# Attention softmax denominators: how the probability blocks are summed before TensorE counts them

## The chip, the cores and the metric

One core of a Trainium2 chip runs one program: a whole decoder layer. The metric is the time of the device in microseconds (us). The kernel before takes 5530.57 us, the median of three runs (5529.32 to 5534.97).

## What is computed

The reference is a decoder layer on x of 2 x 2048 x 512 in float32: self-attention after a layer norm, cross-attention to 77 context rows, and a feed-forward part whose operands are quantised in blocks. The change touches the self-attention alone. It has 16 heads of width 32 and, for every head, two softmaxes with the same queries: a short one with a decay bias and a long one without.

```python
def _attention(q, k, v, bias):
    hd = q.shape[-1]
    scores = jnp.einsum('bhqd,bhkd->bhqk', q, k) / jnp.sqrt(jnp.float32(hd))
    if bias is not None:
        scores = scores + bias[None, None]
    attn = jax.nn.softmax(scores, axis=-1)
    return jnp.einsum('bhqk,bhkd->bhqd', attn, v)
...
decay_bias = -jnp.abs(pos[None, :] - pos[:, None]) * (1.0 - decay_factor)
out_short = _attention(q, k_s, v_s, decay_bias)
out_long = _attention(q, k_l, v_l, None)
out = alpha * out_short + (1.0 - alpha) * out_long
```

With 2 batches, 16 heads and 2 softmaxes there are 64 attention units of 2048 x 2048 scores.

## The kernel before

The program has three stages: the projections (to about 630 us of the span), the attention, which is the function `attend` (about 630 to 4190 us), and the finish (the rest). Only `attend` is changed.

**Units, passes, steps.** A pass has `UNITS` = 4 units (two heads, each with its short and its long softmax), and there are `PASSES` = 16: the first and the last are written out, the others are a hardware loop. A unit has `KB` = 16 blocks of 128 keys, and for each block all 2048 queries stand in `NQ` = 4 chunks of 512. TensorE takes a unit in 16 steps, i = 0 to 15. Each engine has its own instruction stream and runs it in order; they meet at semaphores. A `Rises` object holds a semaphore and how often it rises in a pass.

**One step of TensorE** (the loop over i at the end of the function):
- `times_v(w, n, i)`, L907: the values of block i times its probabilities, into `outputs_T`; first it waits for the exponentials of the block (`expd`).
- `count`, L917, in 6 of the 16 steps: a 128 x 32 tile of ones times a 128 x 2048 tile of summed probabilities, accumulated in `sums`; this is the softmax denominator.
- four `scores_for_exp` (keys by queries, tile `scores_kq`, two banks), for the second half of the next block and the first half of the one after it, and four `scores_for_max` (queries by keys, tile `scores_qk`, three banks) of a later unit, interleaved. The matrix products are at L836.

**The other engines.** ScalarE takes the exponential of each chunk of `scores_kq` into `probs_T` (L745), a ring of `PBUF` = 8 blocks of 128 x 2048 float32. Before it fills a block's buffer again it waits until that block has been used by `times_v` (`summed`) and by the summing (`added`). VectorE reduces each chunk of `scores_qk` to a row maximum (L764), 64 chunks a unit. At the unit's end it negates the maxima (L769), TensorE turns them (`turn_max`, L878), ScalarE rounds them (`round_max`, L719), and SyncE copies them by DMA as one more row of the query operand (`place_max`, L632), where the first `scores_for_exp` of the next unit needs them.

**The summing.** GpSimd adds probability blocks in groups, so that `count` has one tile to multiply in place of two or three:

```python
GROUPS = ((0, 1, 2), (3, 4, 5), (6, 7, 8), (9, 10, 11), (12, 13), (14, 15))
COUNT_LAG = 3
```

A group of three is two adds of 128 x 2048 (L704), a group of two is one: 10 adds and 6 counts a unit. The sum of a group goes to one of two buffers (`probs_group_sum`), and it is counted `COUNT_LAG` = 3 steps after its last block: in steps 5, 8, 11, 14 and, for the last two groups, in steps 0 and 2 of the next unit.

**The end of a unit.** ScalarE copies `sums` out (`take_sums`, L724) when it comes to block 4 of the next unit. VectorE inverts it in four pieces of 128 x 128 (`invert`, L786) in steps 3 to 6 (`INVERT` = 3), multiplies in step 8 (`weigh`, L792) and adds the two softmaxes of a head in step 10 (`mix`, L799). It copies the unit's output out in step 15 (`take`, L781). SyncE stores the mix and, when a unit's last scores are done, loads the operands of the same slot for the next pass (`load`, L619 to L625).

**The maxima's lead.** `ASTEPS` = 12: in steps 0 to 11 the `scores_for_max` and their reductions belong to the last 12 blocks of the next unit, in steps 12 to 15 to the first 4 blocks of the unit after that. The maxima of a unit are thus complete after step 11, and `turn_max` stands in step 12 (`TURN_MAX`). Ahead of the first unit the prologue does all 64 chunks of unit 0 and `EARLY` = 16 chunks of unit 1.

Of the kernel before, what the change touches and what calls it, by code (L numbers as in the profile page):

```python
# [16 lines left out]
F32 = mybir.dt.float32  # L17
# [7 lines left out]
P = 128  # L25
# [487 lines left out]
ASTEPS = 12  # L513

TURN_MAX = 12
INVERT = 3
WEIGH = 8
MIX = 10


GROUPS = ((0, 1, 2), (3, 4, 5), (6, 7, 8), (9, 10, 11), (12, 13), (14, 15))
COUNT_LAG = 3
GROUPS_N = len(GROUPS)
ADDS = KB - GROUPS_N


def adds_until(kb):

    return sum(max(0, sum(b <= max(kb, g[1]) for b in g) - 1) for g in GROUPS if g[0] <= kb)

# [11 lines left out]
def attend(nc, qk_scr, v_scr, gates, kinkA, kinkB, pos_scr, attn_scr):  # L542
# [4 lines left out]
    with ExitStack() as ctx:  # L547
# [10 lines left out]
        group_sum = sb("probs_group_sum", [P, 2, L], F32)  # L558
# [32 lines left out]
        counted = Rises(sem("a_counted"), UNITS * GROUPS_N, credit=1)  # L591
# [89 lines left out]
        def _(pool):  # L681
            give_credit(pool, [maxed, expd, summed, added, counted, taken, sums_out, weighed] + stored)
# [7 lines left out]

            def one_pass(n):
                for w in range(UNITS):
                    for g, blocks in enumerate(GROUPS):

                        wait_apart(pool, counted, counted.at(n, w * GROUPS_N + g - 1), passed)
                        total = group_sum[:, g % 2, :]
                        for b in blocks[1:]:

                            wait_apart(pool, expd, expd.at(n, (w * KB + b + 1) * NQ), passed)
                            first = probs[:, blocks[0] % PBUF, :]  # L700
                            if b > blocks[1]:
                                first = total
                                wait_apart(pool, added, added.at(n, w * ADDS + adds_until(b) - 1), passed)
                            nc.gpsimd.tensor_tensor(total, first, probs[:, b % PBUF, :], ALU.add).then_inc(added.sem, 1)  # L704
# [5 lines left out]
        def _(act):  # L710
# [17 lines left out]
            def one_pass(n, first, last):  # L728
                for w in range(UNITS):
                    back = unit_before(w, n, first)  # L730
                    for kb in range(KB):

                        if back and kb == COUNT_LAG + 1:
# [5 lines left out]
                        old = w * KB + kb - PBUF  # L739
                        act.wait_ge(summed.sem, summed.at(n, old + 1))  # L740
# [649 lines left out]
```

## Time and profile before

The profiled execution took 5527.18 us, of which the span of the profile is 5525.4 us. That is 3.39 us below the median of the three runs.

| | share of the span busy | in the attention |
|---|---|---|
| TensorE | 96% | bound of nearly every step |
| VectorE | 75% | about four fifths |
| ScalarE | 52% | about two thirds |
| GpSimd | 53% | 640 adds of about 4.5 us, otherwise nearly nothing |
| the 16 DMA engines | 11% (by their data queue) | a burst at each unit's end |

How to read the rows: engines are PE (TensorE matrix products), PEld (its weight loads), DVE (VectorE), ACT (ScalarE), POOL (GpSimd) and SP (SyncE, SPq its DMA queue). A name such as L907 is a line of the kernel. In a row of a timeline the first two numbers are start and duration in us, "x8" says how many instructions are merged in it, and the bracket tells how long the engine sat idle before it and what released it. Busy time of PE is not PE at its peak, since matrix products are pipelined.

### The profile page before, as it was taken

What the parts mean: (1) busy time and instruction counts of PE and PEld (TensorE: products, weight loads), DVE (VectorE), ACT (ScalarE), POOL (GpSimd) and SP (SyncE); (2) the same over time, 40 slices, a digit from 0 to 9 for tenths busy, and PEclk for the clock granted to TensorE, in tenths of its full rate; (3) what the DMA queues carried; (4) which work ended last, traced back from release to release, by engine and by line L of the source; (5) the groups of instructions that cost most, each with busy time, mean ns of one, the idle gap of its engine ahead of it and who ended that gap; (6) DMA issues with size and microseconds to landing.
All of it is one profiled execution on the core that took longest, in us unless ns stands there. A gap on an engine that the chain in (4) does not pass through costs nothing. (4 is left out here: it accounts for less than half of the span.)

```text
span 5525.4 us, 97876 instructions
## 1 busy us (share of the span) xinstructions
PE 5303.8 (96%) x28780; PEld 2173.6 (39%) x28780; DVE 4137.8 (75%) x7218; ACT 2882.7 (52%) x5201; POOL 2944.0 (53%) x658
## 2 busy tenths in 40 slices
PE   7999899999999999999999999999996999999999
PEld 3444333333333333333333333333333555555555
DVE  5334688878887888878788878787873777777777
ACT  1111166666666666666666666666663333333332
POOL 0000088888888888888888888888882000000000
PEclk9999799999999999999999999999998999999999
DMA  4332301010101010101001010101001000000000
GB/s 136 107 102 88 92 19 34 21 29 22 34 22 29 22 33 22 29 24 32 25 26 32 24 29 21 34 21 29 21 5 47 23 17 23 17 22 18 17 23 12
DMA packets 145582, 191.11 MB, mean 35 GB/s; under 512 B 18500, under 2 KB 97988, under 8 KB 145030
## 3 DMA queue, kind: packets, MB, share of 16 engines
q1 hardware_dynamic: 145159, 185.65, 11.3%
q8 instruction: 243, 3.98, 0.3%
q14 instruction: 180, 1.47, 0.1%
HBM read 123.56 MB, written 61.64 MB: 34 GB/s over the span
## 5 line engine op out<-in xcount | busy, mean ns | idle before, releaser
L764 DVE TENSOR_REDUCE rowmax_parts<-scores_qk 128x1 f32<-128x512 f32 x4096 | 2529.9, 681 | 642.2 <-PE scores_qk L836 642.2
L745 ACT ACTIVATE probs_T<-scores_kq 128x512 f32<-128x512 f32 x4096 | 2279.8, 597 | 1178.1 <-PE scores_kq L836 1115.7
L704 POOL TENSOR_TENSOR probs_group_sum<-probs_T 128x2048 f32<-128x2048 f32 x384 | 1744.3, 4542 | 563.3 <-ACT probs_T L745 563.3
L836 PE MATMUL scores_kq<-q_operand,k_operand 103*128 103x512 f16 (+3 forms) x3712 | 1274.2, 349 | 10.2 <-ACT probs_T L745 8.3
L704 POOL TENSOR_TENSOR probs_group_sum<-probs_group_sum,probs_T 128x2048 f32<-128x2048 f32 x256 | 1194.4, 4666 | 45.7 <-POOL probs_group_sum L704 45.7
L836 PE MATMUL scores_qk<-k_operand,q_operand 96*128 96x512 f16 (+4 forms) x3712 | 1120.0, 351 | 25.0 <-DMA k_operand<-positions_dram 18.9
L907 PE MATMUL outputs_T<-probs_T,v_operand 128*32 128x512 f32 x8192 | 1093.5, 606 | 28.1 <-issue 24.1
L836 PEld LDWEIGHTS scores_kq<-q_operand,k_operand 103*128 103x128 f16 x3712 | 358.4, 97 | 916.1 <-ACT probs_T L745 522.6
L1339 PE MATMUL f_gate_up<-w_gate_up,xq_T 128*128 128x352 f32 x2048 | 627.3, 462 | 0.8 <-issue 0.8
L836 PEld LDWEIGHTS scores_qk<-k_operand,q_operand 96*128 96x128 f16 (+1 forms) x3712 | 354.5, 98 | 401.2 <-DVE rowmax_parts L764 147.1
L1339 PEld LDWEIGHTS f_gate_up<-w_gate_up,xq_T 128*128 128x128 f32 x2048 | 382.6, 190 | 202.3 <-issue 2.8
L917 PE MATMUL sums<-probs_group_sum,ones 128*32 128x512 f32 x3072 | 415.6, 594 | 13.3 <-issue 10.5
L836 PE MATMUL scores_kq<-q_operand_above,k_operand 103*128 103x512 f16 (+3 forms) x1152 | 398.4, 346 | 0.8 <-ACT probs_T L745 0.6
L836 PE MATMUL scores_qk<-k_operand,q_operand_above 102*128 102x512 f16 (+3 forms) x1152 | 372.8, 352 | 11.1
L473 PE MATMUL products_p<-xn_T,w_qkv 128*128 128x512 f32 x768 | 335.6, 592 | 0.8 <-ACT xn_T L418 0.8
L1328 PE MATMUL f_gate_up<-w_down,hidden_T 128*128 128x512 f32 x704 | 332.5, 599 | 3.4 <-DVE hidden L1247 2.7
L683 POOL MEMSET ones<- 128x32 f32 x1 | 0.1, 125 | 602.4 <-POOLq L213 602.4
L907 PEld LDWEIGHTS outputs_T<-probs_T,v_operand 128*32 128x32 f32 x8192 | 161.3, 108 | 314.1 <-issue 266.6
L786 DVE RECIPROCAL sums_inverse<-sums_T 128x128 f32<-128x128 f32 x256 | 241.0, 943 | 16.2 <-ACT sums_T L724 16.2
L836 PEld LDWEIGHTS scores_kq<-q_operand_above,k_operand 103*128 103x128 f16 x1152 | 110.1, 96 | 345.4 <-ACT probs_T L745 234.1
L494 PE MATMUL products_p<-w_qkv,xn_T 128*128 128x512 f32 x512 | 221.1, 592 | 0.0
L473 PEld LDWEIGHTS products_p<-xn_T,w_qkv 128*128 128x128 f32 x768 | 143.7, 190 | 171.0 <-issue 171.0
(144 smaller groups left out, 3608.2 us busy)
## 6 DMA issues: line engine op xcount, KB each, us to landing
qk_parts_dram<-qk_parts SPq DMA_DIRECT2D x96, 256.0 KB, 2.5
q_operand<-qk_parts_dram SPq DMA_DIRECT2D x192, 128.0 KB, 2.5
k_operand<-qk_parts_dram SPq DMA_DIRECT2D x192, 128.0 KB, 3.0
v_dram<-v_heads SPq DMA_DIRECT2D x16, 1024.0 KB, 5.5
v_operand<-v_dram SPq DMA_DIRECT2D x64, 256.0 KB, 3.3
q_operand_above<-qk_parts_dram SPq DMA_DIRECT2D x96, 128.0 KB, 2.8
x_groups<-x SPq DMA_DIRECT2D x8, 1024.0 KB, 8.8
attention_dram<-o_mixed SPq DMA_DIRECT2D x128, 64.0 KB, 1.6
```

The source lines that it names most:

```text
L473: last = nc.tensor.matmul(mm[:, m % 4, :], w[:, c, m * P:(m + 1) * P], xT[:, u, c, :], start=c == 0, stop=c == KT - 1)
L494: last = nc.tensor.matmul(mm[:, j % 4, :], xT[:, u, c, t * P:(t + 1) * P], w[:, c, (3 + a) * H:(4 + a) * H], start=c == 0, stop=c == KT - 1)
L683: nc.gpsimd.memset(ones[:, :], 1.0).then_inc(consts, 1)
L704: nc.gpsimd.tensor_tensor(total, first, probs[:, b % PBUF, :], ALU.add).then_inc(added.sem, 1)
L745: nc.scalar.activation(probs[:, kb % PBUF, qt * BANK:(qt + 1) * BANK], pb[:, k % 2, :], ACT.Exp)\
L764: nc.vector.reduce_max(rowmax[:, w % 2, c // NQ, c % NQ:c % NQ + 1], pa[:, k % 3, :], AX.X)\
L786: nc.vector.reciprocal(inv[:, r * P:(r + 1) * P], sums[:, r * P:(r + 1) * P]).then_inc(inverted.sem, 1)
L836: return nc.tensor.matmul(out, lhsT, rhs, start=start, stop=stop, skip_group_check=True)
L907: last = nc.tensor.matmul(po[qt * HD:(qt + 1) * HD, :], v_op[:, w, kb, :], probs[:, kb % PBUF, qt * BANK:(qt + 1) * BANK], start=kb == 0, ...
L917: last = nc.tensor.matmul(pc[qt * HD:(qt + 1) * HD, :], ones[:, :], group_sum[:, g % 2, qt * BANK:(qt + 1) * BANK], start=g == 0, stop=g = ...
L1328: last = nc.tensor.matmul(pg[:, 0, 0, :], hT[:, c, :], wd[:, c, :], start=c == 0, stop=c == FT - 1)
L1339: last = nc.tensor.matmul(pg[:, k % 2, g, 0:FW], xqT[:, t, c, :], wgu[:, c, g, k * FW:(k + 1) * FW], start=c == 0, stop=c == KT - 1)
```

## The change

Blocks 0, 1, 3, 5, 7, 9, 11, 13 and 14 of a unit are summed by GpSimd in 8 adds into one tile (two buffers, taken in turn by the units). The other seven are summed by DMAs which GpSimd issues and which add into their destination: chain 0 takes blocks 2, 6 and 10, chain 1 takes blocks 4, 8, 12 and 15. The first DMA of a chain is a plain copy of its block, each later one waits for the one before it and then adds its block. Each moves 128 x 2048 float32, 1 MiB, from one on-chip buffer to another. The three tiles are counted in step 14 (chain 0), step 17, that is step 1 of the next unit (GpSimd's tile), and step 19, that is step 3 of the next unit (chain 1): 3 counts in place of 6.

ScalarE, before it fills a buffer again, waits for the add or for the landing of the DMA that used the block. `take_sums` moves from block 4 to block 5, the inversions from steps 3 to 6 to steps 5 to 8, `weigh` from 8 to 10, `mix` from 10 to 11. `ASTEPS` and `TURN_MAX` go from 12 to 10, which puts `round_max` from block 14 to block 12 and makes `EARLY` 24 chunks in place of 16.

```diff
-ASTEPS = 12
-TURN_MAX = 12
-INVERT = 3
-WEIGH = 8
-MIX = 10
-GROUPS = ((0, 1, 2), (3, 4, 5), (6, 7, 8), (9, 10, 11), (12, 13), (14, 15))
-COUNT_LAG = 3
+ASTEPS = 10
+TURN_MAX = 10
+INVERT = 5
+WEIGH = 10
+MIX = 11
+BY_POOL = (0, 1, 3, 5, 7, 9, 11, 13, 14)
+BY_DMA = ((2, 6, 10), (4, 8, 12, 15))
+ADDS = len(BY_POOL) - 1
+POURS = [len(blocks) for blocks in BY_DMA]
+COUNT_POURED = (14, KB + 3)
+COUNT_ADDED = KB + 1
+TAKE_SUMS = 5
...
+            def add(w, n, b):
+                total = added_sum[:, w % 2, :]
+                wait_apart(pool, expd, expd.at(n, (w * KB + b + 1) * NQ), passed)
+                if b == 1:
+                    first = probs[:, 0, :]
+                    wait_apart(pool, counted, counted.at(n, w - 1), passed)
+                else:
+                    first = total
+                    wait_apart(pool, added, added.at(n, w * ADDS + adds_until(b) - 1), passed)
+                nc.gpsimd.tensor_tensor(total, first, probs[:, b % PBUF, :], ALU.add).then_inc(added.sem, 1)
+            def pour(w, n, b, c):
+                i = BY_DMA[c].index(b)
+                wait_apart(pool, expd, expd.at(n, (w * KB + b + 1) * NQ), passed)
+                if i == 0:
+                    wait_apart(pool, counted_poured[c], counted_poured[c].at(n, w), passed)
+                    nc.gpsimd.dma_start(poured_sum[c][:, :], probs[:, b % PBUF, :]).then_inc(poured[c].sem, 16)
+                else:
+                    wait_apart(pool, poured[c], poured[c].at(n, w * POURS[c] + i), passed)
+                    nc.gpsimd.dma_start(poured_sum[c][:, :], probs[:, b % PBUF, :], accum_op=ALU.add)\
+                        .then_inc(poured[c].sem, 16)
...
+                    for b in range(1, KB):
+                        if b in BY_POOL:
+                            add(w, n, b)
+                        else:
+                            pour(w, n, b, int(b in BY_DMA[1]))
...
-                act.wait_ge(counted.sem, counted.at(n, (w + 1) * GROUPS_N))
+                act.wait_ge(counted_poured[1].sem, counted_poured[1].at(n, w + 1))
...
+                        if b in BY_POOL:
+                            act.wait_ge(added.sem, added.at(n, u * ADDS + adds_until(b)))
+                        elif u >= 0 or not first:
+                            c = int(b in BY_DMA[1])
+                            act.wait_ge(poured[c].sem, poured[c].at(n, u * POURS[c] + BY_DMA[c].index(b) + 1))
...
+            def count_poured(w, n, c):
+                if c == 0:
+                    pe.wait_ge(sums_out.sem, sums_out.at(n, w))
+                pe.wait_ge(poured[c].sem, poured[c].at(n, (w + 1) * POURS[c]))
+                count(poured_sum[c], counted_poured[c], c == 0, c == 1)
+            def count_added(w, n):
+                pe.wait_ge(added.sem, added.at(n, (w + 1) * ADDS))
+                count(added_sum[:, w % 2, :], counted, False, False)
```

## Rows read from the trace of the kernel before

**Rows 1.** The page: busy time, share of span and instructions; then busy tenths.

```profile
PE 5303.8 (96%) x28780; PEld 2173.6 (39%) x28780; DVE 4137.8 (75%) x7218; ACT 2882.7 (52%) x5201; POOL 2944.0 (53%) x658
...
PE   7999899999999999999999999999996999999999
```

**Rows 2.** Windows of 500 us: length, each engine's busy us (instructions), TensorE clock, DMA.

```profile
2000.00:2500.00 500.00, 490.63 (x3242) 165.72 (x3237) 405.62 (x652) 330.00 (x603) 419.00 (x92) 1.00 0.10 27
3500.00:4000.00 500.00, 490.90 (x3233) 164.64 (x3230) 407.34 (x656) 331.17 (x606) 421.22 (x93) 1.00 0.09 26
```

**Rows 3.** Timeline of PE, lines 907 and 917: steps 1 to 6 of a unit.

```profile
2002.50 1.07 PE L907 MATMUL outputs_T<-probs_T,v_operand 128*32 128x512 f32 x8
...
2005.45 1.07 PE L907 MATMUL outputs_T<-probs_T,v_operand 128*32 128x512 f32 x8
2006.34 1.04 PE L917 MATMUL sums<-probs_group_sum,ones 128*32 128x512 f32 x8
...
2009.36 1.06 PE L907 MATMUL outputs_T<-probs_T,v_operand 128*32 128x512 f32 x8
...
2012.56 1.06 PE L907 MATMUL outputs_T<-probs_T,v_operand 128*32 128x512 f32 x8
...
2015.75 1.06 PE L907 MATMUL outputs_T<-probs_T,v_operand 128*32 128x512 f32 x8
...
2019.65 1.06 PE L907 MATMUL outputs_T<-probs_T,v_operand 128*32 128x512 f32 x8
```

**Rows 4.** The page's costliest groups: the counts.

```profile
L917 PE MATMUL sums<-probs_group_sum,ones 128*32 128x512 f32 x3072 | 415.6, 594 | 13.3 <-issue 10.5
```

**Rows 5.** One line, L781, once a unit: duration min/median/max, first and last start.

```profile
L781 DVE COPY o_T<-outputs_T x64: 691/692/693, 744.2 to 4175.1; 128x512 f32<-128x512 f32 x64
```

**Rows 6.** Timeline of DVE in the same steps as Rows 3.

```profile
2007.96 2.48 DVE L764 TENSOR_REDUCE rowmax_parts<-scores_qk 128x1 f32<-128x512 f32 x4 [1.33 <-PE scores_qk L836]
2010.36 0.94 DVE L786 RECIPROCAL sums_inverse<-sums_T 128x128 f32<-128x128 f32 x1
2011.22 2.42 DVE L764 TENSOR_REDUCE rowmax_parts<-scores_qk 128x1 f32<-128x512 f32 x4
2013.55 0.94 DVE L786 RECIPROCAL sums_inverse<-sums_T 128x128 f32<-128x128 f32 x1
```

**Rows 7.** One line, L704, over the attention: duration in ns, first and last start.

```profile
L704 POOL TENSOR_TENSOR probs_group_sum<-probs_T x384: 4517/4543/4557, 696.9 to 4174.0; 128x2048 f32<-128x2048 f32 x192
L704 POOL TENSOR_TENSOR probs_group_sum<-probs_group_sum,probs_T x256: 4515/4538/4978, 701.6 to 4162.6; 128x2048 f32<-128x2048 f32 x128
```

**Rows 8.** Timeline around a unit's end: the maxima's row, and step 15 at 2210.14.

```profile
2202.82 0.24 ACT L719 CAST negmax_T<-turned 16x128 f16<-16x128 f32 x1
...
2203.09 0.53 SPq L632 DMA_DIRECT2D q_operand<-negmax_T  x1
...
2209.86 4.52 POOL L704 TENSOR_TENSOR probs_group_sum<-probs_T 128x2048 f32<-128x2048 f32 x1 [2.21 <-ACT probs_T L745]
...
2210.14 1.06 PE L907 MATMUL outputs_T<-probs_T,v_operand 128*32 128x512 f32 x8
```

**Rows 9.** DMA issues by line: count, KB each, median us from issue to landing.

```profile
v_dram<-v_heads SPq DMA_DIRECT2D x16, 1024.0 KB, 5.5
...
x_groups<-x SPq DMA_DIRECT2D x8, 1024.0 KB, 8.8
...
w_qkv<-L_attn_Wkv_long SPq DMA_DIRECT2D x2, 1024.0 KB, 13.4
...
q_operand<-negmax_T SPq DMA_DIRECT2D x64, 4.0 KB, 1.7
```

**Rows 10.** Window of the loads at the start, and timeline of two DMA issues.

```profile
5.00:20.00 15.00, 0.00 (x0) 0.00 (x0) 14.03 (x16) 0.00 (x0) 0.00 (x0) 1.00 1.04 385
...
619.57 3.92 SPq L340 DMA_DIRECT2D v_dram<-v_heads  x2
629.13 1.28 SPq L619 DMA_DIRECT2D q_operand<-qk_parts_dram  x3
```

**Rows 11.** Timeline: the prologue's 64 reductions, and the attention's last add and count.

```profile
642.01 38.36 DVE L764 TENSOR_REDUCE rowmax_parts<-scores_qk 128x1 f32<-128x512 f32 x64 [8.46 <-PE scores_qk L836]
...
4173.92 1.07 PE L907 MATMUL outputs_T<-probs_T,v_operand 128*32 128x512 f32 x8 [0.96 <-ACT probs_T L745]
4174.05 4.52 POOL L704 TENSOR_TENSOR probs_group_sum<-probs_T 128x2048 f32<-128x2048 f32 x1 [2.08 <-ACT probs_T L745]
...
4178.62 1.07 PE L917 MATMUL sums<-probs_group_sum,ones 128*32 128x512 f32 x8 [2.77 <-POOL probs_group_sum L704]
```

More of the change, by code:

```diff
@@ L511 @@
 MROW = PARTS3 + NPOS
[L513 to L524 removed]
+ASTEPS = 10
[10 more added lines that the diff above has]
+TAKE_SUMS = 5
 def adds_until(kb):
[L529 removed]
+    return max(1, BY_POOL.index(kb))
 def chunks_of(i):
@@ L557, in attend @@
         probs = sb("probs_T", [P, PBUF, L], F32)
-        group_sum = sb("probs_group_sum", [P, 2, L], F32)
+        added_sum = sb("probs_added", [P, 2, L], F32)
+        poured_sum = [sb(f"probs_poured{i}", [P, L], F32) for i in range(2)]
         rowmax = sb("rowmax_parts", [P, 2, KB, NQ], F32)
@@ L590, in attend @@
         added = Rises(sem("a_added"), UNITS * ADDS, credit=1)
-        counted = Rises(sem("a_counted"), UNITS * GROUPS_N, credit=1)
+        poured = [Rises(sem(f"a_poured{i}"), UNITS * POURS[i], 16) for i in range(2)]
+        counted = Rises(sem("a_counted"), UNITS, credit=1)
+        counted_poured = [Rises(sem(f"a_counted_poured{i}"), UNITS, credit=1) for i in range(2)]
         taken = Rises(sem("a_o_taken"), UNITS, credit=1)
@@ L731, in one_pass @@
                     for kb in range(KB):
-                        if back and kb == COUNT_LAG + 1:
+                        if back and kb == TAKE_SUMS:
                             take_sums(*back)
@@ L909, in times_v, with count, counts @@
                 last.then_inc(summed.sem, 1)
-            def count(w, n, g):
-                if g == 0:
-                    pe.wait_ge(sums_out.sem, sums_out.at(n, w))
-                pe.wait_ge(added.sem, added.at(n, w * ADDS + adds_until(GROUPS[g][-1])))
-                for qt in range(NQ):
-                    last = nc.tensor.matmul(pc[qt * HD:(qt + 1) * HD, :], ones[:, :], group_sum[:, g % 2, qt * BANK:(qt + 1) * BANK],
-                                            start=g == 0, stop=g == GROUPS_N - 1)
-                last.then_inc(counted.sem, 1)
+            def count(src, done, first, last):
+                for qt in range(NQ):
+                    mm = nc.tensor.matmul(pc[qt * HD:(qt + 1) * HD, :], ones[:, :], src[:, qt * BANK:(qt + 1) * BANK],
+                                          start=first, stop=last)
+                mm.then_inc(done.sem, 1)
+            def count_poured(w, n, c):
+                if c == 0:
+                    pe.wait_ge(sums_out.sem, sums_out.at(n, w))
+                pe.wait_ge(poured[c].sem, poured[c].at(n, (w + 1) * POURS[c]))
[3 more added lines that the diff above has]
+                count(added_sum[:, w % 2, :], counted, False, False)
+            def counts(w, n, i):
+                for c in range(2):
+                    if i == COUNT_POURED[c]:
+                        count_poured(w, n, c)
+                if i == COUNT_ADDED:
+                    count_added(w, n)
             for c in range(CHUNKS):
@@ L947, in maxima @@
                                 scores_for_max(*unit, chunks[c])
-                        due = [(u, g) for g in range(len(GROUPS)) for u, d in (((w, n), 0), (back, KB))
-                               if u and GROUPS[g][-1] + COUNT_LAG == i + d]
                         times_v(w, n, i)
-                        for u, g in due:
-                            count(*u, g)
+                        counts(w, n, i)
+                        if back:
+                            counts(*back, KB + i)
                         scores(i + 1, 2)
@@ L969, in _ @@
             end = (UNITS - 1, PASSES - 1)
-            for g in range(GROUPS_N):
-                if GROUPS[g][-1] + COUNT_LAG >= KB:
-                    count(*end, g)
+            for i in range(KB):
+                counts(*end, KB + i)
 CTX, CD = 77, 1024
```

17 lines of the change are left out of this document (3 added, 14 removed).

## The prediction

> **What bounds the kernel now.** I read the page first. TensorE is busy for 96% of the span and its row of tenths stays at 9 through the attention [rows 1], so the question is whether a TensorE instruction taken out there is time taken out. The windows of the steady stretch say nearly the same: in 500 us PE is busy 491, DVE 406 to 407, ACT 330 and POOL 419 to 421, at the full granted clock, and the DMA engines are a tenth busy [rows 2]. No engine but PE is close to the bound on average, and the DMA engines are nearly free.
>
> Then the timeline of PE, which is a ruler: each step begins with the eight products of L907. From 2002.50 to 2005.45 is a step without a count, 2.95 us; from 2005.45 to 2009.36 is one with a count, 3.91 us [rows 3]. The count starts 0.89 us after the step and the products after it are moved by its own length. Compared with the usual steps without a count, 2.95 to 3.05, I take 0.87 us for what a count adds. The page's group of the counts gives the same scale: 415.6 us for 3072 products, 8 to a count, so 384 counts of 1.08 us busy each, of which the pipelining hides a part [rows 4]. The first and last of the 64 copies of L781 are 3430.9 us apart [rows 5]; over 63 units that is 54.5 us a unit. Some of it is lost at the loop's back edge; a common unit has 10 steps without and 6 with a count, 10 x 3.05 + 6 x 3.87 = 53.7 us.
>
> Next DVE in the same steps. In the steps that begin at 2009.36 and 2012.56, which last 3.20 and 3.19 us without a count, DVE runs without a gap: an inversion starts at 2010.36, four reductions at 2011.22, the next inversion at 2013.55 [rows 3, 6]. The pitch is 3.19 us: 0.86 for the inversion and 2.33 for four reductions. So these steps, and only these, are set by DVE; PE is late there by 0.15 to 0.25 us.
>
> **The change, part by part.** *Counts taken out.* Three a unit, 192 in all, by 0.87 us: -167 us. All of it lies on the path, since PE sets the steps in which they stand, except what the next paragraph gives back.
>
> *Inversions moved to steps 5 to 8, no count among them.* Before, steps 3, 4 and 6 had no count but step 5 had, and a count step of 3.9 us covers the 3.19 of DVE. Now all four steps last at least 3.19. Four times 0.2 above a step of 2.99, less the 0.45 or so that the old kernel paid in steps 3, 4 and 6, is +0.4 us a unit, +26 us. `weigh` and `mix` (a little under 0.7 us each by the copy of the same shape [rows 5]) make a DVE step of 2.33 + 0.69 = 3.0, about PE's own, so I cost their move at nothing; the cover is thin. The ends are 0 and 1.0 us a unit, the latter if the banks of `scores_qk` never recover between steps 5 and 11. DVE's total is no bound: 406/500 of 54.5 is 44 us of work for a unit.
>
> *GpSimd's adds.* 8 by 4.54 us is 36.3 us a unit where it was 10 [rows 7]. What a DMA issued from GpSimd costs that engine, the trace does not show. The nearest rows are issues from SyncE: 0.43 us each for small ones, 1.96 us each for 1 MiB stores [rows 10]. Nothing makes it less than zero, since the instruction is new. I take 1.2, between them, so 36.3 + 7 x 1.2 = 44.7 of a unit of 51.4 us (53.7 - 2.6 + 0.4 = 51.5; I carry 51.4). GpSimd stays under the bound up to (51.4 - 36.3)/7 = 2.16 us an issue.
>
> *The chains.* This is the part on which the forecast hangs. A block's exponentials are complete about 0.3 us before its step starts: GpSimd was released for block 15 at 2209.86, and step 15 starts at 2210.14 [rows 8]. In the new order GpSimd adds block 11 from 0.3 us before step 11 for 4.54 us, and comes to the DMA of block 12 at 1.2 us after the start of step 12. Steps 12 to 14 (the last with a count) last 10.0 us. Blocks 13 and 14 are two adds in a row, from 0.3 us before step 13, which end 1.9 us after the start of step 15; there GpSimd comes to the DMA of block 15. The count of chain 1 follows `times_v` of step 19, which is 12.9 + 0.9 = 13.8 us after the start of step 15. Let D be the time from when GpSimd begins a DMA to its landing. If D is up to 10.7 the DMA of block 15 is not held by that of block 12, and it lands by 12.6, before 13.8. If D is longer it waits for block 12's, both run in series, and it lands at 2D - 8.8 on that scale, so PE waits 2D - 22.6 us a unit once D is over 11.3. Chain 0 and the other links have four steps, over 12 us, and its count in step 14 comes four steps after block 10, so they bind later.
>
> D has no row of its own. 1 MiB lands in 5.5 us (16 stores), 8.8 us (8 loads of x) and 13.4 us (two weight loads with six others in flight) [rows 9]. An accumulating DMA reads its destination as well. With all engines busy the loads at the start moved 385 GB/s [rows 10], so one more MiB read is 2.7 us. I take 5.5 + 2.7 + 1.2 for the issue, 9.4 us: it fits, with 1.3 us to spare at the link from 12 to 15. I lean to the 5.5 because the stores were packets of a source that stands in the core's memory, as here, and because few other transfers are in flight. The ends are 5.5 and 14.6 (13.4 + 1.2). By the same rate five accumulates (5.4 us) and two copies (2.7 us) keep the DMA engines busy 32.4 us of 51.4, beside the tenth that they were.
>
> The Trainium skill speaks against this part, in "Collectives: The Full Stack", section "The bandwidth ceiling: the fold count and why AG ≠ RS ≠ AR": a reducing DMA has two reads for one write on the same read ring, and so moves data at half the rate of a copy. Applied to the mere extra MiB that is what I have done; applied to the whole of the 8.8 us row it would be 17.6 us, well past 11.3. No row here shows a reducing DMA.
>
> *Buffers and maxima.* ScalarE now waits for a DMA's landing before it fills a buffer, eight blocks later, over 24 us after the block's exponentials: hidden by the ring, unless D passes 20 us. `round_max` ran at 2202.82 and its DMA was issued at 2203.09, to land 1.7 us later, for scores at about 2209.5 in step 14 [rows 8, 9]: some 4.5 us to spare. Two steps earlier makes it over 10; this covers the case that the 4 KB row queues behind a 1 MiB DMA. SyncE's queue has this DMA first, then `store`, then `load`, and none comes later than before, since `mix` moves one step within a unit. `take_sums` comes one block later and its count one step later, so no inversion waits that did not.
>
> *Once per kernel.* The prologue has 8 more reductions at 38.36/64 = 0.6 us: +5 us [rows 11]; what the end of the last pass but one gives back is under 1 us. At the very end the last add was done 4.7 us after the start of step 15, and then came the count [rows 11]. Now block 15's DMA begins at about 2.8 on that scale and lands 9.4 later, 12.2: +8, minus the count of the add that is over by then, so +7 to +9; I take 9.
>
> The sum: -167 + 26 + 5 + 9 = -127 us. The profiled execution took 5527.2 us, so 5400.2; the median stands 3.4 us above it, so **5404 us**. Its own range is 5369 (no loss at DVE, no tail) to 5450 (a loss of 1.0 us a unit there, +38, and a few us for the first and last units).
>
> **The rivals.**
> *The chain lands late (0.22).* This ends slower. The place is the count of chain 1 in step 3 of the next unit. The units give back 2.2 us each and PE waits 2D - 22.6, so it decides at D = 12.4; at the 14.6 of the longest row the wait is 6.6 us a unit, 422 us, and the time 5404 + 422 = 5826. For it: a second read, two chains in flight at once, the 8.8 and 13.4 us rows. Against it: the DMA engines are idle for nine tenths, and the longer rows are loads in a crowd. The skill's rule above, taken in full, is this rival's case.
> *GpSimd becomes the bound (0.09).* An issue over 2.16 us fills it, over (53.7 - 36.3)/7 = 2.49 us it is slower than before. At 3.0 the unit is 57.3 us, 5.9 above 51.4, so 5404 + 378 = 5782. For it: descriptors for 128 rows have to be made by an engine which never made any here. Against it: both issue rows are under 2.
> *Little is gained (0.09).* DVE and a chain that is late by a microsecond eat most of the 2.2 us a unit: 5450 to 5540, about 5490 in the middle. For it: DVE alone sets the inversion steps. Of this, 0.05 is faster and 0.04 within 0.2%.
> That the change does not do what it says would mean that PE does not win the count's time; the two kinds of step, 2.95 and 3.91 us, leave no room for it.
>
> **How the numbers follow.** Forecast 0.60, late chain 0.22, GpSimd 0.09, little gained 0.09. Faster by over 0.2%: 0.60 + 0.05 = 0.65; within 0.2%, about what a measurement of this kernel can tell from no change: 0.04; slower: 0.31. The range: below 5372 I leave 0.03. Above, the late chain reaches 5700 at D = 13.6 and GpSimd at 2.8 us; I put 0.12 of the one and 0.05 of the other beyond. So 5372 to 5700, with 0.20 outside. As both signs have weight: the likeliest case alone has 5369 to 5450.
>
> **What would show it.** Right: copies of L781 about 51.4 us apart, steps of 3.2 us at 5 to 8, the count in step 19 with no wait on a DMA, GpSimd with gaps before most adds, D under 11. Late chain: PE idle before the second poured count, released by a DMA, and GpSimd waiting on a landing before block 15's. GpSimd bound: its adds back to back with the issues, PE waiting on adds or ScalarE on buffers, steps long everywhere. Wrong would be the forecast if D or the issue is out of its bounds, or if GpSimd's adds, 4.54 us with no such DMA beside them, get longer.

## The result and the profile after

The changed kernel takes 5347.05 us (median of four, 5345.61 to 5348.42) against 5530.59: a ratio of 0.9666, 95% interval 0.9652 to 0.9681, or 183.5 us less. The forecast was 5404 us, which is 127 us less, with a range down to 5372. The sign was right, the gain was 57 us larger than forecast, and the measured time lies 25 us below the range. The kernel before took 5528.0 to 5530.6 us (medians) in each of the five sets of runs, so times of different sets are put beside each other as they are.

The page after, busy time and share of span; then the queues (packets, MB, share of 16 engines), and the groups of the DMA issues and their landing (KB each, median us). They answer to [rows 1] and [rows 9]:

```profile
PE 5140.3 (96%) x27244; PEld 2119.3 (40%) x27244; DVE 4123.0 (77%) x7218; ACT 2889.4 (54%) x5201; POOL 2657.0 (50%) x978
...
q0 software_dynamic: 64512, 469.79, 37.8%
q1 hardware_dynamic: 145159, 185.65, 11.5%
...
L718 POOL DMA_DIRECT2D probs_poured<-probs_T x320 | 276.8, 865 | 0.0
...
probs_poured<-probs_T POOLq DMA_DIRECT2D x448, 1024.0 KB, 7.3
```

PE is the bound as before. The DMA engines are busy for 38% of the span more, and issuing an accumulating DMA keeps GpSimd 0.865 us. The line of the page on L718 holds the 320 accumulates; the 128 copies stand at L715. The two lines by themselves, with the time from issue to landing (min/median/max):

```profile
L718 POOL DMA_DIRECT2D probs_poured<-probs_T x320: 826/864/906, 719.1 to 3989.6; - x160
DMA to landing us min/median/max: 6.9/7.6/10.6
```
```profile
L715 POOL DMA_DIRECT2D probs_poured<-probs_T x128: 583/593/738, 706.6 to 3955.2; - x128
DMA to landing us min/median/max: 4.4/4.6/6.0
```

So D, the quantity on which the forecast hung, is 7.6 us (median) for an accumulate and 4.6 for a copy: the accumulate takes 3.0 us more.

The steady window, which answers to [rows 2] (length, PE, PEld, DVE, ACT, POOL busy with instructions, clock, DMA share, GB/s), and one line, the copy that is made once a unit, which answers to [rows 5]:

```profile
2000.00:2500.00 500.00, 494.90 (x3194) 167.02 (x3196) 431.38 (x698) 352.66 (x643) 404.20 (x146) 1.00 0.71 170
```
```profile
L808 DVE COPY o_T<-outputs_T x64: 691/692/694, 747.1 to 3987.9; 128x512 f32<-128x512 f32 x64
```

PE is busy 495 of 500 us, DVE 431, and the DMA share is 0.71 where it was 0.10. From the first to the last of these copies it is 3240.8 us, and was 3430.9.

**Where the 180.8 us of the two spans went.** I took the distance of each of those 64 copies from the next. Common units lasted 53.2 and 54.0 us in turn and now last 51.1 and 51.8. Besides, every fourth unit, the one that holds the back edge of the loop over the passes, lasted 57.4 to 59.5 us and now lasts 52.1 or 52.2. There are 13 such edges. The time in them above a unit of 54.01 or 51.77 us was 55.7 us in all and is 4.8. So:

| part of the span | before | after | difference |
|---|---|---|---|
| to the first copy | 744.2 | 747.1 | +2.9 |
| 13 back edges, above a common unit | 55.7 | 4.8 | -50.9 |
| the 63 units without that | 3375.2 | 3236.0 | -139.2 |
| from the last copy on | 1350.3 | 1356.7 | +6.4 |

The third row is 2.2 us a unit, as forecast. The second row is the part that the forecast did not have. What follows is mostly about it.

### The profile page after: what moved, and what is told of

It reads as the page before. It is cut to its first block and busy times, and to the rows that moved or that the text cites. A ratio compares the mean times of both kernels' runs of the same rounds, so it can differ in the third digit from the quotient of the medians.

```text
span 5344.6 us, 96126 instructions
## 1 busy us (share of the span) xinstructions
PE 5140.3 (96%) x27244; PEld 2119.3 (40%) x27244; DVE 4123.0 (77%) x7218; ACT 2889.4 (54%) x5201; POOL 2657.0 (50%) x978
## 5 line engine op out<-in xcount | busy, mean ns | idle before, releaser
L707 POOL TENSOR_TENSOR probs_added<-probs_added,probs_T 128x2048 f32<-128x2048 f32 x448 | 2030.1, 4532 | 461.0 <-ACT probs_T L772 449.6
L863 PE MATMUL scores_kq<-q_operand,k_operand 103*128 103x512 f16 (+3 forms) x3712 | 1274.6, 349 | 10.6 <-ACT probs_T L772 8.7
L934 PE MATMUL outputs_T<-probs_T,v_operand 128*32 128x512 f32 x8192 | 1091.9, 605 | 4.9 <-ACT probs_T L772 4.9
L707 POOL TENSOR_TENSOR probs_added<-probs_T 128x2048 f32<-128x2048 f32 x64 | 290.3, 4536 | 242.4 <-ACT probs_T L772 242.4
L934 PEld LDWEIGHTS outputs_T<-probs_T,v_operand 128*32 128x32 f32 x8192 | 161.2, 108 | 295.8 <-issue 228.1
L718 POOL DMA_DIRECT2D probs_poured<-probs_T x320 | 276.8, 865 | 0.0
```

The lines of the kernel that those rows point to most:

```text
L718: nc.gpsimd.dma_start(poured_sum[c][:, :], probs[:, b % PBUF, :], accum_op=ALU.add)\
L863: return nc.tensor.matmul(out, lhsT, rhs, start=start, stop=stop, skip_group_check=True)
L934: last = nc.tensor.matmul(po[qt * HD:(qt + 1) * HD, :], v_op[:, w, kb, :], probs[:, kb % PBUF, qt * BANK:(qt + 1) * BANK], start=kb == 0, ...
```

## The experiments

### The back edge: code or work?

Timeline of PE at a back edge of the kernel before, from step 15 (2210.14) to step 1 of the next pass:

```profile
2210.14 1.06 PE L907 MATMUL outputs_T<-probs_T,v_operand 128*32 128x512 f32 x8
2215.48 1.06 PE L907 MATMUL outputs_T<-probs_T,v_operand 128*32 128x512 f32 x8 [2.25 <-issue]
2216.36 1.02 PE L917 MATMUL sums<-probs_group_sum,ones 128*32 128x512 f32 x2
2218.51 1.06 PE L917 MATMUL sums<-probs_group_sum,ones 128*32 128x512 f32 x6 [1.13 <-issue]
2221.47 1.06 PE L907 MATMUL outputs_T<-probs_T,v_operand 128*32 128x512 f32 x8
```

PE waits twice, and for nothing that the profile shows ("issue"): 2.25 us at the edge, and 1.13 us in the middle of a count. The same place in the kernel after:

```profile
2135.80 1.06 PE L934 MATMUL outputs_T<-probs_T,v_operand 128*32 128x512 f32 x8
2139.21 1.07 PE L934 MATMUL outputs_T<-probs_T,v_operand 128*32 128x512 f32 x8 [0.32 <-ACT probs_T L772]
2142.17 1.06 PE L934 MATMUL outputs_T<-probs_T,v_operand 128*32 128x512 f32 x8
```

Both waits on issue are gone. Theory 1: they come from where the loop's instructions lie in TensorE's stream. Theory 2: they come from the work around the edge, which the change also moved (a count in step 0, the maxima, the DMAs).

To place the code I counted TensorE's instructions in the built program, two to a float16 product and four to a float32 one, and took the remainder by 256. The body of the loop begins at 0.82 of such a stretch in the kernel before and its branch stands at 0.09; in the kernel after it is 0.14 and 0.60.

**Padding the kernel before.** The edit is the same in all paddings, with other numbers and, where "hidden", ahead of the prologue, where PE idles while operands load. Two waits are one instruction:

```diff
+            for _ in range(128):
+                pe.wait_ge(consts, 4)
             with nc.Fori(1, PASSES - 1, engines=[pe.engine], hint_back_edge=True) as n:
```

> The kernel before with 64 instructions put into TensorE's stream just ahead of its loop over the passes, each a wait that is already fulfilled; nothing else is changed. Theory 1 (code fetch): in the kernel before, PE stands idle for some 4.4 us at each of the 14 back edges because of where the loop's code lies; by the program the loop body of before begins 0.82 of the way through a stretch of 256 instructions and its branch stands 0.09 into one, in the kernel after it is 0.14 and 0.60. The padding makes it 0.07 and 0.34. Expected: the unit that spans the edge falls from about 58 to 54 us and the time by about 58 us, to 5473 us (the padding itself costs under 10 us). Theory 2 (order of work at the edge: a count in step 0, loads of operands): the padding changes nothing, 5531 to 5540 us.

Measured: 5487.1 us, ratio 0.9923 (0.9906 to 0.9939). The units at the edge last 54.4 or 54.5 us. The unit in which the padding runs lasts 8.8 us longer, 0.14 us an instruction; without it the gain would be 51 us. (The expectations speak of 14 edges; the loop runs 14 times and has 13.) PE at an edge of this kernel:

```profile
2202.67 1.06 PE L907 MATMUL outputs_T<-probs_T,v_operand 128*32 128x512 f32 x8
2206.07 1.06 PE L907 MATMUL outputs_T<-probs_T,v_operand 128*32 128x512 f32 x8 [0.31 <-ACT probs_T L745]
2206.94 1.05 PE L917 MATMUL sums<-probs_group_sum,ones 128*32 128x512 f32 x8
```

It is the old kernel's work in the old order, and both waits are gone. This alone refutes theory 2 for the kernel before.

**Padding the kernel after**, so that its loop begins where that of before does:

> The kernel after with 176 such instructions ahead of TensorE's loop, which puts the beginning of its body at 0.82 of a stretch of 256 instructions, as in the kernel before, and its branch at 0.29. Theory 1 (code fetch): part or all of the wait at the back edge comes back, 1 to 4.4 us at each of 14 edges, so 5347 + 14 to 62 + under 20 for the padding, 5365 to 5420 us; if only the branch's place mattered, it would stay near 5355. Theory 2 (order of work at the edge): no wait at the edge, 5347 to 5360 us.

Measured: 5406.84 us, ratio to before 0.9777 (0.9761 to 0.9793), 60 us above the kernel after. 21.4 us of that are the padding's own unit; the units at the edge now last 53.7 to 57.9 us in place of 52.1 or 52.2, 38 us in all. The wait can be brought into the new kernel by code that does no work. It is 3.3 us an edge here, not 4.3, and stands at another instruction, in the scores behind the first products of the pass:

```profile
2178.49 1.06 PE L934 MATMUL outputs_T<-probs_T,v_operand 128*32 128x512 f32 x8 [0.31 <-ACT probs_T L772]
2181.74 0.39 PE L863 MATMUL scores_kq<-q_operand,k_operand 103*128 103x512 f16 x1 [1.65 <-issue]
```

**The lead of the maxima alone, and 16 instructions alone.** The lead changes the prologue and with it the code's place, by 16 instructions:

```diff
-ASTEPS = 12
+ASTEPS = 10
-TURN_MAX = 12
+TURN_MAX = 10
```

> The kernel before with the maxima's lead of the change alone (ASTEPS and TURN_MAX 10). Theory 1 (code fetch): the loop's code lies at 0.89 and 0.15, much as in the kernel before, so the waits at the back edge stay; the prologue has 8 more reductions, +5 us: 5536 us (5531 to 5541). Theory 2 (order of work at the edge): the work of the edge is moved with the maxima, which should take away a part of the wait, up to 58 us: down to 5478 us. The prediction on record costed this part at +5 us.

Measured: 5493.34 us, ratio 0.9935 (0.9918 to 0.9952). The edge units fell to 54.9 to 55.3. That was a miss: I had called 0.89 and 0.15 as bad as 0.82 and 0.09. Either the lead's work mattered, or 16 instructions did, so I shifted the kernel before by 16 hidden instructions:

> The kernel before with 16 already fulfilled waits in TensorE's stream ahead of the prologue, where TensorE waits for loads anyway, so they cost nothing. They put the loop's code where the run with the maxima's lead alone has it (0.89 and 0.15 of a stretch of 256 instructions, in place of 0.82 and 0.09). In that run the wait at the back edge fell from 4.2 to 1.1 us, which the theory of the code's place did not foresee. Theory 1a (place of the code, and 16 instructions decide): the unit at the edge is 55.1 us, the time 5530 - 13 x 3.1 = 5489 us. Theory 2 (the lead's own work at the edge): the unit stays at 58 us and the time at 5530 us.

Measured: 5493.4 us, ratio 0.9937 (0.992 to 0.9953), the same as the lead's. The edge units last 55.0 to 55.7 us, but for two at 57.6 and 57.9. So it was the 16 instructions. The two kernels differ only by the lead's work. Their common units are alike to 0.03 us. The lead's kernel makes its first copy 5.9 us later (longer prologue) and spends 7.9 us less in the edges, so in sum the lead itself is worth nothing there. One such edge:

```profile
2197.95 1.07 PE L908 MATMUL outputs_T<-probs_T,v_operand 128*32 128x512 f32 x8
2202.56 1.07 PE L908 MATMUL outputs_T<-probs_T,v_operand 128*32 128x512 f32 x8 [1.52 <-ACT probs_T L745]
2203.43 1.05 PE L918 MATMUL sums<-probs_group_sum,ones 128*32 128x512 f32 x8
```

The profile puts this wait down to ScalarE, but only 0.3 of the 1.52 us can be ScalarE's: from the start of the exponentials before it (2199.37) to these products it is 3.19 us here, and 1.97 us in the run with 64 of padding.

**A shift of 256.** If any padding helped, the stretch of 256 would be a fancy of mine:

> The kernel before with 256 already fulfilled waits in TensorE's stream ahead of the prologue. They move the loop's code by a whole stretch of 256 instructions, so it lies as in the kernel before within one (0.82 and 0.09). If the place within a stretch of 256 decides: the unit at the edge is 57.5 to 58.7 us again, as in the kernel before, and the time is 5530 plus once some 25 us for the padding (0.13 us each, of which about 8 us are hidden): 5545 to 5565 us. If any padding helps, or the distance to something else in the program counts: the unit at the edge is 54.4 to 55.6 us and the time about 5505 us.

Measured: 5551.24 us, ratio 1.0036 (1.0022 to 1.005). The edge units are 58.1 to 61.4 us, 5.0 above a common one, and the two waits are back in their old places. (Here the padding is not hidden in full: the first copy comes 21.0 us later than before.)

```profile
2235.26 1.06 PE L908 MATMUL outputs_T<-probs_T,v_operand 128*32 128x512 f32 x8
2240.20 1.06 PE L908 MATMUL outputs_T<-probs_T,v_operand 128*32 128x512 f32 x8 [1.85 <-issue]
2241.08 1.02 PE L918 MATMUL sums<-probs_group_sum,ones 128*32 128x512 f32 x2
2243.23 1.06 PE L918 MATMUL sums<-probs_group_sum,ones 128*32 128x512 f32 x6 [1.13 <-issue]
```

A shift of 16 or 64 takes most of the wait away and one of 256 does not, so the place within a stretch of 256 instructions matters. (A stretch of 128 would fit these three shifts as well.) The profile has a queue of instruction transfers, of 16 KB each; the kernel before made 243 of them, that with 64 of padding 230, the kernel after 214:

```profile
q8 instruction: 243, 3.98, 0.3%
```
```profile
q8 instruction: 230, 3.77, 0.3%
```
```profile
q8 instruction: 214, 3.51, 0.2%
```

From 243 to 230 is 13, as many as there are edges. The times of these transfers tell more. At the edge shown for the kernel before, one runs from 2212.50 to 2213.60 and another from 2215.84 to 2217.10; PE starts again at 2215.48 and at 2218.51. At the edge of the kernel with 64 of padding they run from 2200.70 to 2201.69 and from 2206.76 to 2207.74, and PE's longest wait there is 0.31 us. I set every wait of PE from 1 us before to 9 us after the copies at the 13 edges beside the last transfer that ended before the wait did, in all 14 traces:

| kernel | loop begins, branch | waits over 0.5 us | from the transfer's end to the wait's end, us |
|---|---|---|---|
| before | 0.82, 0.09 | 24 | 1.2 to 1.9 |
| before, shifted by 256 | 0.82, 0.09 | 22 | 1.3 to 2.0 |
| before, lead alone | 0.89, 0.15 | 13 | 1.7 to 2.0 |
| before, shifted by 16 | 0.89, 0.15 | 13 | 1.8 to 2.1 |
| after, shifted by 176 | 0.82, 0.29 | 13 | 1.3 to 1.7 |
| two counts a unit (below) | 0.88, 0.09 | 13 | 1.7 to 2.0 |
| one chain (below) | 0.13, 0.34 | 11 | 1.8 to 2.0 |
| the other seven, the kernel after among them | | 0 | no wait over 0.43 us |

In the seven without waits the last transfer had ended 3.3 us or more before PE started. The run with one chain tells place and lateness apart, since all its edges have the same code: at 11 of them a transfer ends 1.4 to 2.0 us after the copy and PE waits 1.3 to 1.9 us, at the other two it ends 0.7 and 1.0 us before the copy and PE waits 0.33. So PE waits for code that is fetched late, and the place of the loop's code is one thing that makes the fetch late. What else does (that run lies at the good place of the last kernel below) is not settled.

### The price of the counts

```diff
-                for qt in range(NQ):
+                for qt in range(NQ) if g in (0, 2, 5) else ():
                     last = nc.tensor.matmul(pc[qt * HD:(qt + 1) * HD, :], ones[:, :], group_sum[:, g % 2, qt * BANK:(qt + 1) * BANK],
                                             start=g == 0, stop=g == GROUPS_N - 1)
-                last.then_inc(counted.sem, 1)
+                if g in (0, 2, 5):
+                    last.then_inc(counted.sem, 1)
+                else:
+                    pe.sem_inc(counted.sem, 1)
```

> The kernel before without the products of three of its six counts (those of the second, fourth and fifth group); the groups are still added, so this leaves part of the denominators out and shows the price of three counts alone. The loop's code lies at 0.18 and 0.74. Theory of the record: 192 counts by 0.87 us are 167 us; the inversions stay in steps 3 to 6, of which step 5 loses its count, so a little is given back: a common pair of units of 53.2 and 54.0 us falls by 2.4 to 2.6 us each. With theory 1 (code fetch) the waits at the back edge go as well, 58 us: 5531 - 160 - 58 = 5313 us. With theory 2 (order of work at the edge; the count in step 0 is among those left out) also 5313 us or so; without either 5371.

Measured: 5317.76 us, ratio 0.9616 (0.96 to 0.9632). Common units last 50.8 and 51.4 us, 2.4 and 2.6 less than before, and the edge units 51.8 or 51.9. So three counts are worth 2.5 us a unit by themselves, 0.84 each. (The expectation has one thing wrong: the counts left out are those of steps 8, 14 and 0, and step 5 keeps its own, so nothing is given back there.) The kernel after, which has the same number of counts, is at 51.1 and 51.8: the rest of the change, the later inversions and the DMAs above all, costs 0.3 us a unit.

### The chains

**Half the slack.** Chain 1 counted one step earlier:

```diff
-COUNT_POURED = (14, KB + 3)
+COUNT_POURED = (14, KB + 2)
```

> The kernel after with chain 1 counted in step 18 in place of 19. In the profile after, block 15's DMA is issued at 2087.00 and lands 7.6 us later, at 2094.6; step 18 begins at 2094.47 and its count would come at 2095.4, step 19 begins at 2097.40. By this reading 0.8 us are to spare: no wait in common units, 5345 to 5352 us. If landings next to a unit's loads are later than that: 0.3 to 1 us a unit, 5365 to 5410 us.

Measured: 5366.59 us, ratio to before 0.9701 (0.9686 to 0.9716), 20 us above the kernel after. Half the units are as they were (51.8); the others last 51.4 to 52.2 in place of 51.1. The counts' line says what for (idle before it, times): first this kernel, then the kernel after.

```profile
  DMA probs_poured<-probs_T: 81.4, 92
```
```profile
  DMA probs_poured<-probs_T: 12.2, 4
```

My reading of 0.8 us to spare was wrong: it took the median of all accumulates, 7.6 us, for the DMA of block 15. In the steady passes of the kernel after that DMA takes 7.3 to 10.6 us; its medians over the four units of a pass are 8.9, 7.6, 9.0 and 8.5, so in half the units it is late for step 18 as a rule. In step 19 there are 3 us more, and that is enough.

**One chain in place of two.**

```diff
-BY_DMA = ((2, 6, 10), (4, 8, 12, 15))
+BY_DMA = ((), (2, 4, 6, 8, 10, 12, 15))
-COUNT_POURED = (14, KB + 3)
+COUNT_POURED = (None, KB + 3)
```

> The kernel after with all seven DMA blocks in one chain, GpSimd's tile counted in step 17 and the chain in step 19, so two counts a unit; 64 hidden waits put the loop's code at 0.13 and 0.34. Nothing is left out. The record's model of the chain: an accumulating DMA lands 7.6 us after its issue but a link comes every two steps, 6.1 us. From the first DMA: 4.6 + 4 x 7.7 + 10.2 (two adds) + 7.6 to the last landing, then the count, then the next unit's first DMA: 54 to 56 us a unit where two chains would allow 50.5, so 5293 + 64 x 4 to 5.5 = 5550 to 5645 us. Rival: landings overlap enough that one chain hides as two do: 5285 to 5300 us.

Measured: 5845.16 us, ratio 1.0563 (1.0547 to 1.0579): slower than the kernel before. Units last from 50.2 to 69 us. GpSimd waits for a landing before the next link, and TensorE waits for GpSimd. GpSimd in the middle of a unit, and PE at the count in step 17:

```profile
2039.46 0.88 POOL L718 DMA_DIRECT2D probs_poured<-probs_T  x1 [2.65 <-DMA probs_poured<-probs_T]
2040.07 4.83 POOL L707 TENSOR_TENSOR probs_added<-probs_added,probs_T 128x2048 f32<-128x2048 f32 x1
2048.34 0.88 POOL L718 DMA_DIRECT2D probs_poured<-probs_T  x1 [3.44 <-DMA probs_poured<-probs_T]
```
```profile
2050.56 1.06 PE L935 MATMUL outputs_T<-probs_T,v_operand 128*32 128x512 f32 x8
2058.49 1.93 PE L942 MATMUL sums<-probs_added,ones 128*32 128x512 f32 x8 [6.87 <-POOL probs_added L707]
```

The two links shown are 8.9 us apart where the blocks come every 6.1 (in this unit 7.6 to 10.0). The mechanism of the late chain exists, with the landing time that the kernel after has (here a median of 7.5). The size was off by 200 us or more: I had priced the chain's own count and forgotten that the waits for landings also hold the adds queued behind them on GpSimd, whose total is counted two steps sooner. A part of it is the clock. After the wait of 6.87 us the granted TensorE clock was 0.50, and the count took 1.93 us in place of 1.04:

```profile
2058.50:2064.00 5.50, 5.50 (x20) 1.46 (x21) 2.30 (x4) 1.79 (x3) 5.29 (x2) 0.50 0.82 167
```

Between 750 us and the last copy this run has 65 such stretches, 474 us in all, with PE busy for 309 of them; the kernel after has none. At the full clock the 309 us would be about half, so my estimate is that up to 155 us of the miss are the clock's.

### The maxima's lead, beside the DMAs

```diff
-ASTEPS = 10
+ASTEPS = 12
-TURN_MAX = 10
+TURN_MAX = 12
```

> The kernel after with the maxima's lead of before (ASTEPS and TURN_MAX 12). In the profile after, the 4 KB DMA of the maxima lands 6.0 us after its issue, not 1.7 as before, since 1 MiB DMAs are in flight. Before there were some 4.5 us to spare. Theory 3 (the earlier maxima pay only beside the DMAs): TensorE waits for that DMA at the end of step 14, 1 to 3 us in most units, 5347 - 5 + 64 to 190 = 5406 to 5530 us. Rival: the products queued ahead of the scores hide it, no wait, 5342 us. The code's place (0.07 and 0.54) is a good one by theory 1.

Measured: 5381.11 us, ratio to before 0.9735 (0.9719 to 0.9751), 34 us above the kernel after. It is 25 us under the range that I gave, and of the mechanism named. The wait stands at the end of step 14, where the unit's first scores need the row of the maxima:

```profile
2041.23 0.23 PE L863 MATMUL scores_kq<-q_operand,k_operand 103*128 103x128 f16 x1 [0.92 <-DMA q_operand_above<-negmax_T]
```

For every second unit the row goes to two tiles, by two 4 KB DMAs. Here they were issued at 2033.97 and 2034.56 and landed at 2039.85 and 2041.11; PE was ready at 2040.31, so it is the second that it waited for. The time to landing of such DMAs, in the kernel before and in the kernel after (in this run 1.7/6.3/7.4):

```profile
DMA to landing us min/median/max: 1.6/1.7/3.6
```
```profile
DMA to landing us min/median/max: 1.7/5.8/6.5
```

So this part of the change is worth nothing without the DMAs (the pair of runs above), and 34 us with them: 41 us in the units, less 5 for the longer prologue and 2 at the end.

### Variations on the kernel after

**Inversions in every other step** (5, 7, 9, 11; weighing in 12, mix in 13):

```diff
-                        if back and INVERT <= i < INVERT + NQ:
-                            invert(*back, i - INVERT)
+                        if back and i in range(INVERT, INVERT + 2 * NQ, 2):
+                            invert(*back, (i - INVERT) // 2)
```

> The kernel after with the four inversions in steps 5, 7, 9 and 11 in place of 5 to 8, the weighing in step 12 and the mix in 13. In the profile after, steps 5 to 8 last 3.19 to 3.26 us where VectorE has no gap. If VectorE sets these steps and recovers in between: 0.3 to 0.6 us a unit, 5347 - 19 to 38 = 5309 to 5328 us. If each single inversion still makes its step 3.2 us long (no backlog is carried over), no gain: 5345 to 5350 us.

Measured: 5337.95 us, ratio to before 0.9655 (0.9639 to 0.9672). Common units fall by 0.14 and 0.18 us. This is between the two expectations. Each step with an inversion still lasts 3.2 us, wherever it stands. The gain is mostly that of step 10: with the weighing in it, beside the turning of the maxima, it lasts 3.25 or 3.31 us in the kernel after, and here, without the weighing, 2.96 or 3.14.

**Two counts a unit.** GpSimd adds chain 0's total to its own after block 15:

```diff
+                    total = added_sum[:, w % 2, :]
+                    wait_apart(pool, poured[0], poured[0].at(n, (w + 1) * POURS[0]), passed)
+                    wait_apart(pool, added, added.at(n, (w + 1) * ADDS - 1), passed)
+                    nc.gpsimd.tensor_tensor(total, total, poured_sum[0][:, :], ALU.add).then_inc(added.sem, 1)
```

> The kernel after with one count fewer: GpSimd adds the total of chain 0 to its own sum after the DMA of block 15 (9 adds a unit), this sum is counted in step 18, chain 1 in step 19. Nothing is left out. By the price of a count that the record has (0.87 us) and the one that the run without three counts gives (0.83): common units of 51.1 and 51.8 us fall by 0.8 to 0.9 us. The loop's code comes to 0.88 and 0.09, by theory 1 a bad place: 1 to 4.4 us are lost at each of 13 edges, so 5347 - 54 + 13 to 57 = 5306 to 5350 us. By theory 2 no loss: 5293 us.

Measured: 5323.99 us, ratio to before 0.9632 (0.9616 to 0.9648). Common units last 50.2 and 50.9 us, 0.9 less, which is a count's price. The edge units last 51.9 to 54.9: 30 us above a common unit in all, where the kernel after had 4.8. So nearly half of what the count saved (54 us) is lost there again, as the code's place foretold.

**All of it, in a good place**: two counts, spread inversions, and 64 hidden instructions.

> Two counts a unit (as in the run with one count fewer), the inversions in steps 5, 7, 9 and 11, and 64 already fulfilled waits in TensorE's stream ahead of the prologue, where it idles, so that the loop's code comes to 0.13 and 0.34. Nothing is left out. If the code's place makes the waits at the edge: they fall from 1 to 4 us to about 0.4, some 38 us in all, and 5324 - 38 - 9 = 5277 us (5270 to 5285). If the third count covered something at the edge: 5300 to 5315 us.

Measured: 5289.65 us, ratio to before 0.9564 (0.9551 to 0.9577). The edge units are at 51.4, common ones at 50.0 and 50.9. The waits at the edge went, as expected, but the time is 5 us above the range given for that: they had cost 30 us in the run before this one and cost 6 here, so 24 us came back, not 38. And spreading the inversions shortened only every second unit; in the other, step 14 now lasts 3.20 us in place of 3.02, and there a weight load of TensorE waits 0.49 us for VectorE. It computes all that the reference asks and is the fastest of the kernels run.

## Why the prediction was wrong, and where it was right

**The step that failed** is in "What bounds the kernel now": "Some of it is lost at the loop's back edge; a common unit has 10 steps without and 6 with a count". The mean of 54.5 us a unit [rows 5] and the 53.7 of a common one stand side by side there. The difference, 0.8 us over 63 units, is about 50 us. I named it, looked no further and carried it as a constant, so it has neither a row nor a term in the sum. It was 4.3 us at each of 13 edges, in waits that end 1.2 to 1.9 us after a transfer of instructions, and the change took 50.9 us of the 55.7 away, with no line of it meant to. The bounds were drawn from the costs of the change's parts alone; an idle time that nothing in the program explains should have been in them, from 0 to -56 us, which would have put the measured time inside.

**Counts taken out.** -2.6 us a unit forecast, 2.5 by the run with three counts left out. Right.

**Inversions moved.** +0.4 forecast. The steps 5 to 8 of the profile after last 3.19 to 3.26 us. The DVE timeline answers to [rows 6]:

```profile
2053.77 0.94 DVE L813 RECIPROCAL sums_inverse<-sums_T 128x128 f32<-128x128 f32 x1
2054.63 2.42 DVE L791 TENSOR_REDUCE rowmax_parts<-scores_qk 128x1 f32<-128x512 f32 x4
2056.96 0.94 DVE L813 RECIPROCAL sums_inverse<-sums_T 128x128 f32<-128x128 f32 x1
```

It is 3.19 us from one inversion to the next. Against the run with three counts left out a unit pays 0.3 us for all moves and the DMAs together. Right in size. But the move of `weigh`, costed at nothing with a thin cover, is in it: step 10 lasts 3.25 or 3.31 us, as the run with the spread inversions tells. `weigh` takes 0.74 us, not a little under 0.7.

**GpSimd.** An issue costs 0.86 us (0.59 for a copy), 0.79 in the mean, forecast 1.2 with a bound of 2.16. With adds of 4.53 us it has gaps of 0.8 to 2.7 us before most of them (median 1.0). Right in kind, forecast half as dear again as it is.

**The chains.** D was put at 9.4 and is 7.6 in the median; for the DMA of block 15, on which the forecast hung, it is 7.6 to 9.0 by unit, up to 10.6, and so just under the 10.7 that the forecast allowed. The extra read was put at 2.7 us; the accumulate takes 3.0 more than the copy. In the steady passes the count of step 19 never waits for a DMA; it does at the attention's very end, for 4.95 us. The Trainium skill's rule of two reads for one write ("Collectives: The Full Stack", "The bandwidth ceiling: the fold count and why AG ≠ RS ≠ AR") agrees with 4.6 against 7.6 us if 1.6 us of each are fixed, which no run here shows; applied to a whole load row of 8.8 us, 17.6, it would have misled. The rivals of a late chain and of a full GpSimd did not come about, but the run with one chain shows how near the first is.

**Buffers and maxima.** Forecast as a cover for a 4 KB row that queues behind 1 MiB DMAs: it does, 5.8 us for 1.7, and the cover is worth 34 us. The text gave the old order 4.5 us to spare behind a landing of 1.7, some 6.2 from the issue on; it had not counted the second DMA, issued 0.6 us later, whose landing in the run with the old lead took 6.6 us at the place shown.

**Once per kernel.** Forecast +5 and +9, measured +2.9 and +6.4. The lead alone moved the first copy by 6.0 us (744.2 to 750.2); the first unit has three counts fewer, by 0.84 us each (an estimate from the run above) 2.5 us.

Without the back edges the sum comes to -129.9 us (-139.2 + 2.9 + 6.4), and the forecast was -127. The terms were right in sum, with small errors that cancel; one that was not among them made the miss. That the change moved the code to a good place was luck: nothing in it aimed there, and taking one more count out moved it to a bad one.

## What to carry to other kernels

Divide the span by the number of rounds and compare it with a common round; if they differ, find the rounds that are longer before pricing anything, since an edit of any kind can move what makes them long. A wait on "issue" at a loop's edge is tested by a few dozen idle instructions put ahead of the loop: here 64 gave 43 us, a quarter of what the whole change gave. When DMAs are to take over an engine's work, price the small DMAs that now travel beside them, and give a landing a due time by the rows of that very DMA: the median of its line hid one that was over 1 us slower in half the units.

## What the runs showed of the hardware that I had not expected

- At the back edge of a loop of some 3100 to 3400 TensorE instructions PE can wait for its code: 109 waits of 0.5 us or more, in seven kernels, all end 1.2 to 2.1 us after a 16 KB instruction transfer has ended. The profile says "issue" for them, or names an engine that was done before.
- The size of this goes with the code's place within a stretch of 256 instructions: 4.3 us an edge at 0.82/0.09 and 5.0 after a shift of 256, 1.1 to 1.7 us after a shift of 16, 0.4 after one of 64. The place is counted from the built program; where such a stretch truly begins is not known.
- An instruction that holds two already fulfilled waits costs TensorE 0.12 to 0.14 us (8.8 us for 64, 21.4 us for 176).
- An accumulating DMA of 1 MiB within the core's memory lands 7.6 us after its issue (median), a copy 4.6; five and two of them in 51 us keep the DMA engines 0.71 busy and slow neither TensorE's products (605 ns, 606 before, at L934 and L907) nor GpSimd's adds (4.53 us, 4.54 before), but make a 4 KB DMA 4 us and a 256 KB load 3 us slower (6.3 for 3.3).
